# Moving the first turnings behind the attention products, the values' bias to their eviction, and small sums to GpSimd

## The reference

```python
# layer 0, h = relu(layernorm(x)), N x 256; adj is N x N of 0 and 1
attn_a = sigmoid(concat([adj @ h, h]) @ Wa.T + ba)      # attn_b likewise with Wb
hd = h @ W_sa
e = where(adj != 0, exp(-leaky_relu(s_left[:, None] + s_right[None, :], 0.01)), 0)
x_a = (e / (sum(e) + 1e-5)) @ hd
x_b = adj @ (h @ W_gcnb) + b_gcnb
x = x + sigmoid(attn_a * x_a + attn_b * x_b)
# layer 1, h = relu(layernorm(x)), 32 graphs of 64 nodes, mask = same graph
scores = (where(mask, q @ k.T / 16, 0) + adj + adj) * where(mask, 1, -1e6)
x = x + (softmax(scores) * mask) @ (h @ Wv.T + bv)
```

## Time and profile before

| | |
|---|---|
| median of 3 runs | 272.99 us (272.70 to 273.46) |
| profiled execution | 275.27 us |
| its span | 273.5 us, granted clock 0.951 in the mean |
| TensorE busy | 233.1 us (85%) |
| VectorE busy | 196.3 us (72%) |
| ScalarE busy | 157.3 us (58%) |
| GpSimd busy | 50.9 us (19%) |

### The profile page before, as it was taken

How to read it: one execution, slowest core, us unless ns; L and a number is a source line. 1 busy time by engine, 2 the same in 40 slices (tenths; PEclk the granted TensorE clock), 3 DMA queues, 4 the chain that set the end, 5 groups by cost and what they waited for, 6 DMA issues and landing times.

```text
span 273.5 us, 5362 instructions
## 1 busy us (share of the span) xinstructions
PE 233.1 (85%) x2032; PEld 196.1 (72%) x2032; DVE 196.3 (72%) x503; ACT 157.3 (58%) x301; POOL 50.9 (19%) x85
## 2 busy tenths in 40 slices
PE   0687999979998999999999999999269987799832
PEld 0567887769786888888888888878147866578621
DVE  3587777986675677799936999459942458978951
ACT  3557727974546683947529567188634446466520
POOL 2533300000020000011000110001200004675794
PEclk9999999999799999999999999999759999979975
DMA  5998096009894001742200000000000000111112
GB/s 180 364 388 264 6 385 226 2 12 343 250 322 153 0 2 24 285 153 65 90 2 1 4 0 2 0 2 0 0 0 2 0 4 0 35 46 38 57 62 80
DMA packets 20091, 26.34 MB, mean 96 GB/s; under 512 B 1888, under 2 KB 11872, under 8 KB 20064
## 3 DMA queue, kind: packets, MB, share of 16 engines
q1 hardware_dynamic: 19376, 25.71, 27.4%
q10 hardware_dynamic: 688, 0.27, 0.4%
HBM read 23.88 MB, written 2.10 MB: 95 GB/s over the span
## 4 chain that ended last, share of the span: by engine, by line
PE 58%; DVE 13%; ACT 10%; POOL 9%; issue 6%; DMA 2%; POOLq 0%; DVEq 0%; ACTq 0%
PE bank_b L942 19%; PE bank_a L966 9%; PE bank_a L968 9%; PE bank_a L970 8%; PE bank_a L890 5%; POOL adjt L554 5%; POOL adjt L559 3%; ACT e_slot L615 2%; PE bank_l L890 2%; DVE e_lo L1453 2%; DMA e_slot<-in_gate_w 2%; PE bank_b L890 1%; PE bank_l L882 1%; DVE x_all L1618 1%; DVE st6b L1623 1%
## 5 line engine op out<-in xcount | busy, mean ns | idle before, releaser
L966 PE MATMUL bank_a<-hd,e_hi 128*128 128x257 f16 x256 | 70.7, 276 | 0.6 <-ACT xa L684 0.6
L968 PE MATMUL bank_a<-hd,e_hi 128*128 128x257 f16 x256 | 71.1, 278 | 0.0
L970 PE MATMUL bank_a<-hd,e_lo 128*128 128x257 f16 x256 | 70.3, 275 | 0.0
L942 PE MATMUL bank_b<-hb,adjt 128*128 128x259 f16 (+1 forms) x512 | 67.6, 276 | 0.2 <-DVE xb L1439 0.2
L942 PEld LDWEIGHTS bank_b<-hb,adjt 128*128 128x128 bf16 x512 | 49.8, 98 | 7.8 <-DVE xb L1439 0.5
L622 ACT ACTIVATE e_hi<-e_slot 128x1024 f16<-128x1024 f32 x32 | 33.7, 1054 | 37.5 <-PE bank_a L970 23.6
L1453 DVE SCALAR_TENSOR_TENSOR e_lo<-e_slot,e_hi 128x1024 f16<-128x1024 f32 x32 | 39.0, 1220 | 11.1 <-ACT e_hi L622 11.1
L1447 DVE SCALAR_TENSOR_TENSOR e_slot<-e_slot,adjt 128x1024 f32<-128x1024 f32 x32 | 39.0, 1220 | 9.2 <-ACT e_slot L615 9.2
L615 ACT ACTIVATE e_slot<-s_row,nbias 128x512 f32<-128x512 f32 x64 | 42.5, 713 | 0.3
L540 POOL TENSOR_TENSOR rs_all<-veb,half_neg 128x2 f32<-128x2 f32 x8 | 7.3, 918 | 143.4 <-DVE veb L1628 143.4
L966 PEld LDWEIGHTS bank_a<-hd,e_hi 128*128 128x128 f16 x256 | 25.1, 98 | 5.1 <-issue 0.7
(11 more groups left out here) (211 smaller groups left out, 370.9 us busy)
## 6 DMA issues: line engine op xcount, KB each, us to landing
adjt<-in_adj_t SPq DMA_DIRECT2D x16, 1024.0 KB, 7.5
x_all<-in_x SPq DMA_DIRECT2D x4, 512.0 KB, 5.4
out<-adjt SPq DMA_DIRECT2D x16, 128.0 KB, 1.8
adjt<-in_x SPq DMA_DIRECT2D x3, 512.0 KB, 8.0
diag<-in_adj SPq DMA_DIRECT2D x16, 64.0 KB, 3.6
adjt<-in_x SPq DMA_DIRECT2D x2, 256.0 KB, 3.8
e_slot<-in_L_gnn_W_gcnb ACTq DMA_DIRECT2D x1, 256.0 KB, 3.9
e_slot<-in_W_saT SPq DMA_DIRECT2D x1, 256.0 KB, 4.3
```

The source lines that it names most:

```text
L942: eng.matmul(B[:, r % 2, 0:cols], adjt_block(k, j, r), hb16[:, j, part, 0:cols], start=(j == 0 and part == 0), stop=(j == NT - 1 and part ...
L966: eng.matmul(A[:, r, 0:D + 1], high, hd16[:, j, 0, 0:D + 1], start=(j == 0), stop=False, skip_group_check=True)
L968: eng.matmul(A[:, r, 0:D + 1], high, hd16[:, j, 1, 0:D + 1], start=False, stop=False, skip_group_check=True)
L970: mm = eng.matmul(A[:, r, 0:D + 1], low, hd16[:, j, 0, 0:D + 1], start=False, stop=(j == NT - 1), skip_group_check=True)
```

## The change

In each engine's list:

- **Head.** VectorE's `moments(2)` and `shift(2)` and GpSimd's `inv_deviation(2)` go behind the steps that make the gate columns; the norm of W_sa is summed one pair later (g == 3) and its scaling follows one later on ScalarE and VectorE; a_col is loaded from SyncE's queue instead of ScalarE's; in ScalarE's and VectorE's lists the halves of hd go ahead of `raw`, `high`, `mask` and `low`.
- **Last block.** `turn_h1(0)` moves from step 4 to step 5, `keys(0)` from 5 to 6, `values(0)`, `turn_h1(1)` and `keys(1)` to 7, and `values(1)`, `turn_h1(2)`, `keys(2)` and `values(2)` behind the attention products. ScalarE's and VectorE's lists follow; `add_mix` of the last block goes wholly ahead of the loop over p.
- **Values.** VectorE's `keep_values` evicts values plus scaled bias to `v32` (float32, SBUF). ScalarE makes the high half and GpSimd the low one from there. `with_bias` is gone, and `results` multiplies by the reciprocal of the scaled sum and adds x1. bias² enters the norm of the values.
- **Row sums.** `off_a` and the row's sum are made on GpSimd; VectorE keeps the reciprocal.
- **Banks.** `gather(6)` and `gather(7)` write the two banks of the values, and wait for the last `lift` instead of results.

```diff
@@ sync
             load_batch(0)
+            eng.dma_start(a_lr[:, :, :], a_col).then_inc(w4_loaded, 16)
             load_batch(1)
@@ gpsimd
             inv_norm(0, 1, 1)
+            inv_norm(1, 7, 2)
             inv_deviation(2)
-            inv_norm(1, 7, 2)
-            def with_bias(p):
...
+            def values_low(p):
+                eng.wait_ge(v_hi_made, p + 1)
+                eng.tensor_tensor(v16[:, p % 4, :, 1, :], v32[:, p % 2, :, :], v16[:, p % 4, :, 0, :], ALU.subtract) \
+                   .then_inc(v_lo_made, 1)
+
+            def outer_part(p):
+                eng.wait_ge(row_b_ready, p + 1)
+                eng.tensor_tensor(off_a[:, 2 * p:2 * p + 2], row_b[:, 2 * p:2 * p + 2], lift[:, 2 * p:2 * p + 2],
+                                  ALU.subtract).then_inc(off_a_ready, 1)
+
+            def row_sums(p):
+                own = slice(2 * p, 2 * p + 2)
+                eng.wait_ge(fo_ready, p + 1)
+                eng.tensor_tensor(z_out[:, own], z_off[:, own], fo[:, own], ALU.mult).then_inc(zs_ready, 1)
...
+                eng.tensor_tensor(z_out[:, own], z_out[:, own], zw[:, own], ALU.add).then_inc(zs_ready, 1)
...
+                eng.tensor_scalar(zs[:, own], z_out[:, own], v_inv[:, 0:1], None, ALU.mult).then_inc(zs_ready, 1)
...
+            for p in range(3):
+                values_low(p)
+            inv_new_deviation(NT - 4, NT - 2)
+            outer_part(0)
             inv_new_deviation(NT - 2, NT)
+            row_sums(0)
+            for p in range(3, NQ):
+                outer_part(p - 2)
+                row_sums(p - 2)
+                values_low(p)
+            for p in (NQ - 2, NQ - 1):
+                outer_part(p)
+                row_sums(p)
@@ scalar
-            eng.dma_start(a_lr[:, :, :], a_col).then_inc(w4_loaded, 16)
...
+            hd_high(2)
             raw(0)
-            hd_high(2)
+            hd_high(3)
             raw(1)
+            hd_high(4)
             high(0)
-            hd_high(3)
             keep_row(2)
+            hd_high(5)
             raw(2)
+            hd_high(6)
             high(1)
+            hd_high(7)
+            raw(3)
+            high(2)
             keep_row(3)
             eng.wait_ge(rows_kept, NC)
-            raw(3)
-            hd_high(4)
-            hd_high(5)
-            high(2)
-            hd_high(6)
-            hd_high(7)
...
             def values_high(p):
-                eng.wait_ge(v_summed, p + 1)
+                eng.wait_ge(v_kept, p + 1)
                 wait(eng, pv_summed, p - 3)
-                eng.activation(v16[:, p % 4, :, 0, :], VALUES[:, :, 0:D], ACT.Copy).then_inc(v_hi_made, 1)
+                eng.activation(v16[:, p % 4, :, 0, :], v32[:, p % 2, :, :], ACT.Copy).then_inc(v_hi_made, 1)
...
+                        eng.activation(bv_s[:, :], bv_row[:, 0:D], ACT.Square, accum_out=bv_sq[:, 0:1]) \
+                           .then_inc(sq_1_made, 1)
...
+            keys_high(1)
             keep_a(LAST, 0, CT)
+            values_high(1)
+            h1T_high(2)
+            tanh_mix(LAST, 0, 2)
+            keys_high(2)
+            tanh_mix(LAST, 2, CT)
+            values_high(2)
             h1T_high(3)
-            tanh_mix(LAST, 0, 2)
             exponents(0, 0)
             exponents(0, 1)
-            tanh_mix(LAST, 2, CT)
@@ tensor
-                if g == 2:
+                if g == 3:
                     eng.wait_ge(sq_made, 2)
-                    eng.matmul(A[:, 1, 2 * D - 1:2 * D], ones[:, :], sq[:, 7:8], start=True, stop=True) \
+                    eng.matmul(A[:, 3, 2 * D - 1:2 * D], ones[:, :], sq[:, 7:8], start=True, stop=True) \
...
                 if p == 0:
                     eng.wait_ge(a_kept, NT)
+                elif p < NQ - 2:
+                    eng.wait_ge(o_ready, 2 * p)
                 else:
-                    eng.wait_ge(o_ready, 2 * p)
+                    eng.wait_ge(lift_ready, NQ)
...
                 if k == LAST:
-                    if q == 4 and place == 0:
+                    if q == 5 and place == 2:
                         turn_h1(0)
-                    if q in (5, 6, 7) and place == 0:
-                        keys(q - 5)
-                    if q in (5, 6, 7) and place == 2:
-                        values(q - 5, 0)
-                        values(q - 5, 1)
-                        if q < 7:
-                            turn_h1(q - 4)
+                    if q == 6 and place == 2:
+                        keys(0)
+                    if q == 7 and place == 0:
+                        values(0, 0)
+                        values(0, 1)
+                        turn_h1(1)
+                    if q == 7 and place == 2:
+                        keys(1)
...
+            values(1, 0)
+            values(1, 1)
+            turn_h1(2)
+            keys(2)
+            values(2, 0)
+            values(2, 1)
             turn_h1(3)
             scores(0)
             scores(1)
@@ vector
-            moments(2)
             eng.wait_ge(norm_summed, 2)
...
             hT_low(0)
-            shift(2)
+            moments(2)
...
             hT_low(1)
+            shift(2)
             moments(3)
...
+            def keep_values(p):
+                eng.wait_ge(v_summed, p + 1)
...
+                wait(eng, v_lo_made, p - 1)
+                eng.tensor_tensor(v32[:, p % 2, :, :], VALUES[:, :, 0:D], across(bv_s[:, :], [P, 2, D]), ALU.add) \
+                   .then_inc(v_kept, 1)
...
             def results(p):
+                own = slice(2 * p, 2 * p + 2)
+                eng.wait_ge(zs_ready, 3 * p + 3)
+                eng.reciprocal(rz[:, own], zs[:, own]).then_inc(rz_ready, 1)
+                eng.wait_ge(rz_ready, p + 1)
                 eng.wait_ge(pv_summed, p + 1)
...
-                    eng.scalar_tensor_tensor(out=o_sb[:, p, n, :], in0=RESULTS[:, n * D:(n + 1) * D],
-                                             scalar=rzv[:, i:i + 1], in1=xo[:, p % 2, n, :],
+                    eng.scalar_tensor_tensor(out=o_sb[:, p, n, :], in0=result_bank(p)[:, n * D:(n + 1) * D],
+                                             scalar=rz[:, i:i + 1], in1=x1_all[:, i * D:(i + 1) * D],
...
+            keys_low(1)
             denominators(LAST, 0, CT)
             mix(LAST, 0)
             mix(LAST, 1)
-            h1T_low(3)
+            keep_values(1)
+            h1T_low(2)
             mix(LAST, 2)
             mix(LAST, 3)
+            keys_low(2)
+            keep_values(2)
+            h1T_low(3)
+            add_mix(LAST, 0, 2)
             maxima(0)
-            add_mix(LAST, 0, 2)
+            add_mix(LAST, 2, CT)
+            shifts(CT * LAST, CT * LAST + 2)
             for p in range(3, NQ):
                 maxima(p - 2)
                 if p >= 4:
-                    row_sums(p - 3)
                     results(p - 4)
...
-                values_low(p)
+                keep_values(p)
```

More of the change, by code:

```diff
@@ L414, in score_bank, with result_bank @@
             return A[:, p % 3, :]
-        RESULTS = A[:, 3, :]
+        def result_bank(p):
+            return A[:, 3, :] if p < NQ - 2 else B[:, p - NQ + 2, :]
         @block.sync
@@ L562, in _ @@
-            for i in range(0, NT - 2, 2):
-                inv_new_deviation(i, i + 2)
-            eng.wait_ge(scale_1_made, 10)
-            eng.wait_ge(mask_ready, PAIRS)
-            eng.wait_ge(b_summed, NT)
-            with_bias(0)
-            inv_new_deviation(NT - 2, NT)
-            for p in range(1, NQ):
-                with_bias(p)
+            def values_low(p):
+                eng.wait_ge(v_hi_made, p + 1)
+                eng.tensor_tensor(v16[:, p % 4, :, 1, :], v32[:, p % 2, :, :], v16[:, p % 4, :, 0, :], ALU.subtract) \
+                   .then_inc(v_lo_made, 1)
@@ new lines, in _ @@
+            for i in range(0, NT - CT, 2):
+                inv_new_deviation(i, i + 2)
+            eng.wait_ge(scale_1_made, SCALES)
+            for p in range(3):
+                values_low(p)
+            inv_new_deviation(NT - 4, NT - 2)
+            outer_part(0)
+            inv_new_deviation(NT - 2, NT)
+            row_sums(0)
[6 more added lines that the diff above has]
+                row_sums(p)
@@ L826, in _ @@
                 values_high(p)
-                if p in (4, 5):
-                    normalize(p + 2)
-            exponents(NQ - 2, 0)
-            exponents(NQ - 2, 1)
+                if p in (3, 4):
+                    normalize(p + 3)
             pT_high(NQ - 3)
-            exponents(NQ - 1, 0)
-            exponents(NQ - 1, 1)
+            for p in (NQ - 2, NQ - 1):
+                exponents(p, 0)
+                exponents(p, 1)
             pT_high(NQ - 2)
@@ L1375, in _ @@
                     shift(g + 3)
-                if g == 2:
+                if g == 3:
                     eng.wait_ge(norm_summed, 3)
-                    eng.wait_ge(hb_hi_made, 3)
-                    eng.tensor_scalar(norm_sq[:, 7:8], A[:, 1, 2 * D - 1:2 * D], TINY, None, ALU.add) \
```

(39 more changed lines are left out.)

92 lines of the change are left out of this document (29 added, 63 removed).

## The result

| | before | after |
|---|---|---|
| median | 273.23 us (272.70 to 273.75, 4 runs) | 261.37 us (260.41 to 261.98, 4 runs) |
| profiled execution | 275.27 us, span 273.5, clock 0.951 | 260.9 us, span 259.1, clock 0.991 |

The ratio of after to before is 0.956, 95% interval 0.952 to 0.960. By the medians that is 11.9 us faster, where 11.8 was forecast. The two profiled executions lie 14.4 us apart, because that of before was 2.0 over its median and that of after 0.5 under it. The sum of the prediction is a sum over profiles, so its terms are held against those 14.4.

The account below looks back on a forecast made before the run. TensorE, busy 85% of the span, was the engine to follow, its idle time in head, middle and tail. Gains 0.9 + 0.7 + 1.8 + 3.5 + 4.9 = 11.8 us put the median at 261.3, range 257.6 to 266.5.

Parts of the forecast that it names:

- head, first tile product: Start of the head: moments(2) and inv_deviation(2) moved behind the gate columns' steps start the first tile product 0.9 us earlier.
- whole head, loop entry: From the start to the main loop's entry: 0.9 (start), 0.7 (square of W_sa) and 1.8 us (hd) gained.
- main loop: Main loop: added small operations run while TensorE has work; cost 0, at most 1 us if one were exposed.
- middle, h1T_low(0) to gather(4): Last block: stall moved, not removed, and shorter gather steps; gain 3.5 us if the clock falls again, 5.2 if not.
- tail: From gather(4) to the last result: GpSimd's bias sums and the gathers' wait for results go; gain 4.9 us.
- GpSimd: Middle: values_low takes 1.4 us, at worst 2.3, hidden in a step of 5.3; blocking of VectorE taken as 0.
- (a): Rival, middle: the clock holds through the second stall, 1.7 us less, 259.6; chance 0.15.
- (b): Rival, middle: bare round trips after the last attention product eat its gain, so it gives 0: 264.7 us; chance 0.22.
- (c): Rival, head: it gives 1, not 3.4, as ScalarE limits it: 263.7 us, or 267.2 without the middle; chance 0.13.
- (d): Rival, gather steps: values_low on GpSimd blocks VectorE; at the upper price 6.6 us slower, 279.6; chance 0.04.
- (e): Rival, whole kernel: the moved stalls cancel head and tail and nothing shows, 273 us; chance 0.03.

Follow-up runs that it names:

- old_head: Kernel after with the head of before (moments(2), W_sa norm, a_col load, order of hd's halves): 265.02 us, ratio 0.969 to the kernel before.
- before_head: Kernel before with the head edits alone: 270.86 us, ratio 0.989 to the kernel before.
- clock_held: Kernel after with 24 useless TensorE products into a free bank ahead of keys(0) in the last block: 261.29 us, ratio 0.956 to the kernel before.
- counts_late: Kernel after with the last block's counts behind h1T_low(0) on VectorE and h1T_high(0) ahead of normalize(2) and (3) on ScalarE: 259.02 us, ratio 0.945.
- low_on_vector: Kernel after with values_low on VectorE instead of GpSimd: 261.56 us, ratio 0.954 to the kernel before.
- one_bank: Kernel after with gathers 6 and 7 writing the common bank again and waiting for results: 263.83 us, ratio 0.964 to the kernel before.
- before_banks: Kernel before with only gathers 6 and 7 in the values' banks: 274.58 us, ratio 1.001 to the kernel before.
- old_turns: Kernel after with the last block's turnings, keys, values of pairs 0 to 2 and add_mix where before had them: 265.85 us, ratio 0.970.
- turn_first: Kernel after with h1T_high(2) ahead of keep_a, values_high(1) (ScalarE), and keep_values(1), h1T_low(2) ahead of mix(0), mix(1) (VectorE): 260.81 us, ratio 0.948.
- both: Kernel after with the edits of counts_late and turn_first together: 256.10 us, ratio 0.933 to the kernel before.

## Why the prediction was right, point by point

The forecast median was 261.3 and the measured one 261.4. That it agrees to 0.1 is luck in part, as the terms show (gain in the profiles; where the place is a TensorE row, by its starts):

| term | forecast | measured |
|---|---|---|
| head, first tile product | 0.9 | 14.48 - 13.96 = 0.5 |
| whole head, loop entry | 3.4 | 62.45 - 59.17 = 3.3 |
| main loop | 0 | 1.65 |
| middle, h1T_low(0) to gather(4) | 3.5, or 5.2 if the clock holds | 4.5 |
| tail | 4.9 | 14.22 - 9.27 = 4.95 |
| sum | 11.8 | 14.4 |

(Main loop: VectorE's h1T_low(0) started at 200.09 before and at 195.16 after, 4.93 earlier, of which 3.28 is the head's. Middle: 256.21 - 246.77 - 4.93.)

- **Head: right in sum, one bound too small.** No wait for the square, hd_low no longer waited for, and keep_row(3) is what TensorE waits for before the loop (1.02 us), as walked; old_head and before_head confirm the sum from both sides. The term of the start was mis-sized in this pair of profiles, 0.5 and not 0.9 (the rest of the head gave 2.8 and not 2.5), by a step that the prediction put at 0 with a bound of 0.3: a_col in SyncE's queue delays the loads behind it, and TensorE now waits 0.66 for W_saT. In the eleven profiles with this head that wait is 0 in five and 0.25 to 1.2 in six. The first tile product starts at 12.96 to 13.38 where there is no such wait and at 13.33 to 14.54 where there is one; in the three profiles with the old head there is none, and it starts at 14.10 to 14.48. In none of them did a_col alone go back to ScalarE's queue, so that it is this move and not the load's own spread is argued and not shown.
- **Main loop: not foreseen, and mostly not the change's.** 1.65 us are the half clock of 69 to 73, which this execution of before had. The clock falls there in executions of either head. By its size it is also most of the 2.0 us by which before's profiled execution, with a mean clock of 0.951, lay over its median. Of the 31 runs of before in the three groups ten had 0.951 or 0.952 and took 274.8 to 275.9 us; the 21 with 0.954 to 0.963 took 273.0 to 274.4. So it is in the profiles' 14.4 and hardly in the medians' 11.9; where in the program those ten lost their clock no trace tells. Head, middle and tail measured 12.7; before's other 0.4 over its median and the 0.5 by which after's execution lay under its own bring that to 11.8. So the forecast median is right to 0.1 with a middle that was 1.0 too small: this error and the distances of the two profiled executions from their medians nearly cancelled, which is luck.
- **Middle: the mechanism right, the clock half wrong.** The stall was moved, not removed: 2.76 before keys(0) (2.9 forecast), 0.89 before keys(1) (0.7), 3.31 before keys(2) (3.4), with keys(0) to keys(2) 16.33 us (16.47). The clock fell after the first and held through the second, where the prediction took a second fall as likelier and put 1.7 us on it. keys(2) to gather(0) took 13.4 where 12.9 was walked for a clock that holds, and the steps were 5.4, 5.4, 5.4 and 4.8. So 4.5 lies between the two forecasts. clock_held shows that the second fall was a real case and not a wrong mechanism: with the same second stall it came. counts_late shows the other case, also with no fall before it. What decides between them stays open.
- **GpSimd: right.** values_low takes 1.16 us (1.4 forecast from half the shape), no L1689 is over 0.223 us, TensorE nowhere waits for GpSimd, and low_on_vector makes no difference. The blocking by which the case of a slower kernel would have come never happened; in the tail the two begin close together (L1689 at 247.43, L547 at 247.55), in the order that was walked, and in none of the ten profiles with values_low on GpSimd does that operation begin inside an L547. The risk itself was real, and the prediction had overlooked its best row. In the kernel before, L1666 did once begin inside GpSimd's sum and took 0.57 us instead of 0.22. In the kernel after it is a GpSimd operation that waits: L552 takes 0.20, and 0.43 where it begins inside VectorE's L1636, 220.44 to 221.13.

```profile
256.06 1.40 POOL L559 TENSOR_TENSOR adjt<-adjt,x_all 128x256 f32<-128x256 f32 x2
256.91 0.57 DVE L1666 SCALAR_TENSOR_TENSOR st<-st,s_post,lift 128x2 f32<-128x2 f32 x1
...
220.09 0.70 POOL L542 TENSOR_TENSOR rs_all<-veb,half_neg 128x2 f32<-128x2 f32 x1 [2.00 <-DVE veb L1646]
...
220.31 0.22 DVE L1689 SCALAR_TENSOR_TENSOR st<-st,s_post,lift 128x2 f32<-128x2 f32 x1
...
220.44 0.69 DVE L1636 SCALAR_TENSOR_TENSOR x_all<-xa,x_all 128x512 f32<-128x512 f32 x1
...
220.75 0.43 POOL L552 TENSOR_TENSOR st<-st,lift 128x2 f32<-128x2 f32 x1
```

(The first two are of the kernel before, the other four of the kernel after.) By the rule of the Trainium skill (SBUF — State Buffer, SBUF: two separate sides) it is the operation that begins first that keeps the other out. L1666 and L552 agree with it, one in each direction; the power L542 does not: L1689 and L1636 begin inside it and take their usual time. So the rule is a warning to look at the rows, and not yet a price.

- **Tail: right to 0.05.** Gathers 6 and 7 wait for the probabilities and no longer for results; gather(5), which has no bank of its own, waits 0.69 for results(4). one_bank and before_banks show that the banks are worth nothing without the move of the bias, and 2.2 with it.
- **The rivals.** (a), the clock holding through the second stall, is what the profiles of this kernel show, and the middle gave most of what it said, 4.5 of 5.2. (b), the middle giving nothing, falls by old_turns: 4.2 us worse. (c), a head of 1 us, falls by old_head and before_head. (d) and (e) fall by the result.

## What to carry to other kernels

Subtract the profile's own bad luck before summing: where the granted clock is at half in a stretch that the engine fills, the profiled execution is no typical one, and a term in it will "gain" without being touched. A stall that is moved to where three engines answer each other can be shortened again by asking of each list what stands ahead of the one piece that TensorE waits for; here two such moves gave 4.8 us by the medians (5.8 by the ratios), as much as the whole middle of the change. And a bank or buffer of its own is worth only what the next wait behind it leaves: measure it with and without that wait.

## What the runs showed of the hardware

- TensorE's clock after a stall isn't settled by that stall. Behind the same 3.3 us of idle time it held in the kernel after, fell in the one whose first stall had been filled with work (clock_held), and held in the one whose first stall was 0.73 us (counts_late). In one execution of before it was at 0.57 with TensorE busy in all of 69 to 73 us.
- One fall of the clock on the way costs 1.65 us: from keys(0) to values(0) it was 4.29 us with the fall and 2.64 without (clock_held).
- A GpSimd subtraction of 128x512 with float16 result took 1.16 us in each of eight in the kernel after, and wasn't stretched there beside VectorE, unlike the power of before; in turn_first and in both one of the eight took 1.26 and 1.27.
- A VectorE operation that begins inside a GpSimd one can end with it, and the other way round: 0.57 us instead of 0.22 (L1666 in the kernel before), 0.43 instead of 0.20 (L552 in the kernel after). Inside GpSimd's power (L542, 0.70) it doesn't wait: L1689 took its 0.22 there.
